# Fewer turns of the identity on the tensor engine in the set-up of a fused decoder layer

## The reference, cut to what matters

```python
x = x + attn(layernorm(x), W_attn, b_attn, W_proj, b_proj)      # 16 heads of 8, rotary factor on q and k, causal
x = x + xattn(ctx, ctx, layernorm(x), Wk, Wv, bv, Wq, bq, Wo, bo)
x = x + ffn(layernorm(x), router_w, w_gate, w_up, w_down, sw_gate, sw_up, sw_down, gate_w)
```

## Time and profile before

| what | us |
|---|---|
| median of 3 runs | 470.13 |
| lowest and highest of the 3 | 468.83, 485.78 |
| the profiled execution's own time | 470.84 |
| its span, first to last instruction | 469.1 |
| PE busy in the span | 407.7 (87%) |
| DVE, ACT, POOL busy | 335.8, 294.8, 258.9 |
| mean granted clock of TensorE | 0.955 |

### The profile page before, as it was taken

One profiled execution on the slowest core, in us unless ns is written; L12 is line 12 of the kernel. 1 busy time (PEld: TensorE's weight loads), 2 busy tenths in 40 slices (PEclk: granted clock), 3 DMA queues, 4 the chain that ended last, 5 costly groups with the idle time before them and its releaser, 6 DMA issues. The chain is left out here.

```text
span 469.1 us, 14511 instructions
## 1 busy us (share of the span) xinstructions
PE 407.7 (87%) x4932; PEld 321.6 (69%) x4932; DVE 335.8 (72%) x1125; ACT 294.8 (63%) x989; POOL 258.9 (55%) x313
## 2 busy tenths in 40 slices
PE   8987999989989898898987866988888889989884
PEld 7655777767667676676666644777777777767673
DVE  6266678899988988878877565856566566656467
ACT  2156699898979889788977654464454444534320
POOL 7834071544857758655445647654555555555453
PEclk9999699999999999999999785899999999999998
DMA  7423022221422313214011261223222323232198
GB/s 200 142 67 138 3 96 79 98 94 44 149 70 69 124 33 115 84 47 146 28 31 42 75 199 47 65 61 77 73 76 76 86 71 79 71 83 61 41 296 241
DMA packets 46712, 43.15 MB, mean 92 GB/s; under 512 B 6320, under 2 KB 38336, under 8 KB 46640
## 3 DMA queue, kind: packets, MB, share of 16 engines
q1 hardware_dynamic: 41150, 32.70, 22.8%
q0 software_dynamic: 4320, 8.99, 5.7%
q10 hardware_dynamic: 1170, 0.53, 0.4%
HBM read 17.26 MB, written 12.09 MB: 63 GB/s over the span
## 5 line engine op out<-in xcount | busy, mean ns | idle before, releaser
L701 POOL DMA_INDIRECT ys<-ctx_t,xload x71 | 68.2, 960 | 57.3 <-ACT ctx_t L1277 41.2
L657 POOL DMA_INDIRECT xs<-xrow,posu x64 | 66.8, 1044 | 21.4 <-issue 11.5
L1159 ACT ACTIVATE probs<-ps_scores 128x512 f32<-128x512 f32 x128 | 72.0, 599 | 3.3 <-PE ps_scores L840 3.3
L1023 PE MATMUL ps_scores<-wide,xe 128*128 x213 | 66.9, 423 | 1.8 <-DVE xe L1589 1.8
L683 POOL TENSOR_SCALAR xrow<-res,mv,rs 128x128 f32<-128x128 f32 x27 | 21.7, 804 | 75.7 <-ACT rs L1207 75.6
L1600 DVE COPY probs<-ps_shared 128x256 f32<-128x256 f32 x71 | 30.0, 423 | 37.9 <-PE ps_shared L1031 23.8
L1382 DVE TENSOR_REDUCE negmax<-ps_scores 128x4 f32<-128x512 f32 x64 | 41.1, 684 | 17.4 <-PE ps_scores L810 16.8
L1267 ACT ACTIVATE xe<-ps_scores 128x128 fp32r<-128x128 f32 x71 | 19.6, 278 | 40.5 <-PE ps_scores L1015 21.6
L1040 PE MATMUL ps_shared<-wd,probs 128*128 x284 | 43.9, 277 | 0.1
L1382 DVE TENSOR_REDUCE negmax<-s_copy 128x4 f32<-128x512 f32 x64 | 42.8, 673 | 0.3 <-ACT s_copy L1153 0.3
L1272 ACT ACTIVATE vst<-ps_scores 128x256 f32<-128x256 f32 x71 | 27.4, 386 | 24.8 <-PE ps_scores L1023 21.4
(11 more groups left out here) (250 smaller groups left out, 1094.3 us busy)
## 6 DMA issues: line engine op xcount, KB each, us to landing
wide<-x_late SPq DMA_DIRECT2D x42, 256.0 KB, 2.5
xload<-xs SPq DMA_DIRECT2D x71, 66.0 KB
wide<-ys SPq DMA_DIRECT2D x8, 512.0 KB, 7.3
ctx_t<-in_ctx SPq DMA_DIRECT2D x32, 64.0 KB
out_x<-res SPq DMA_DIRECT2D x8, 256.0 KB, 3.7
wide<-x_late SPq DMA_DIRECT2D x6, 192.0 KB, 2.3
ys<-ctx_t,xload POOLq DMA_INDIRECT x71
wd<-in_L_ffn_w_down SPq DMA_DIRECT2D x8, 128.0 KB
```

Of the source, the lines that this page charges most:

```text
L657: pool.indirect_dma_start(out=xs, out_offset=bass.IndirectOffsetOnAxis(ap=posu[:, g % 2, k, u:u + 1], axis=0), in_=xrow[:, g % 2, k, u, :] ...
L701: pool.indirect_dma_start(out=ys, out_offset=bass.IndirectOffsetOnAxis(ap=xload_i[:, i % XL, C + 1:C + 2], axis=0), in_=ybuf[:, i % 4, :], ...
L1023: mm = pe.matmul(PS[i % 2][:], a[:, i % 4, :], m[:, bass.ds(e, 1), :].rearrange("p a f -> p (a f)"), start=(r == 0), stop=(r == 2))
L1159: act.activation(probs[:, b % 2, j * HJ:(j + 1) * HJ, :].rearrange("p a t -> p (a t)"), SC[score_bank(("scores_t", b), j)][:], ACT.Exp)\
```

## The change

It shortens two of the rows of identity turns and takes the third away, with the function that only the third used. Nothing else is moved, and no wait is added or taken away.

```diff
-            def free_turns(bank, n):
-
-                for _ in range(n):
-                    pe.transpose(bank[:, 0:128], ident[:], ident[:])
-
...
                 if g == 0 and n == 1:
                     turned_weights()
-                    idle_turns(8)
+                    idle_turns(2)
...
                 if b == 0:
-                    idle_turns(18)
+                    idle_turns(3)
...
                 bank = w.bank_free(("turn_max", b))
-                if b == 0:
-                    free_turns(bank, 14)
                 w.ge(maxed, NJ * (b + 1))
                 pe.transpose(bank[0:NH, 0:T], negmax[:, b % 2, :], ident[:]).then_inc(put_bank(("turn_max", b)), 1)
```

## The result

The changed kernel takes 478.57 us in the median of 4 runs (475.69 to 480.09), the kernel before, run beside it, 470.37 (4 runs). The ratio is 1.0186, 95% interval 1.0126 to 1.0246: slower, by 8 us, against the 6.2 forecast. (A ratio compares only the runs in the faster and more frequent of two states that executions fall into; of the four runs before, the one of 485.78 us is not in it.) Repeats of the whole change gave 1.0135 (1.0082 to 1.0188), 1.0128 (1.0082 to 1.0173) and 1.0115 (1.0053 to 1.0176). They ran on two other chips, on both of which the same kernel before takes 436 to 437 us (the last slots of its pipeline take 6.5 instead of 7.4 us; slots 5 to 14 are the same, and the slots before them differ only with the clock), so absolute times are compared only inside one set of runs.

The account below looks back on a forecast made before the run. It took the early slots' serial loop of TensorE bursts and ACT exponentials as the bound, run at the low clock: 2.0 us late at the exponentials, +2.4 and +1.8 in two slots, sum +6.2, giving 476.3 us, range 468.4 to 483.0.

Parts of the forecast that it names:

- scores(0) at 20.75: First scores burst, set-up: starts about 20.75 instead of 22.24 us, once the six stack moves land at 20.6.
- turn_max(0) at 25.75: Turn of the first row maxima: starts at 25.75 instead of 26.57 us, 0.8 us sooner.
- Which execution: Set-up: step times taken from the one profiled execution, its clock rising at some 21.1 us.
- The one-and-a-half microseconds of part two: Second row cut, 18 to 3 turns, ahead of scores(0): lets it start 1.5 us sooner.
- The folded biases at 0.42 us each: Between turn_max(0) and scores_t(0): four starts 0.42 us apart, 1.7 us together, the same at either clock level.
- The low level through slot 3, and slot 4 at the low level too: Low clock from scores(0) through slot 3, costing +2.4 and +1.8 us in two slots; slot 4 unchanged, 0.
- Part three: Removing the 14 turns before turn_max(0), which started 0.5 us after the maxima were there.
- The first clock record comes after 45 us: Sign that the forecast is right: the trace's first recorded clock change comes after 45 us.
- Rival (a): Early slots: the clock comes up anyway or holds, leaving only the 0.9 us ordering gain, 469.2 us; chance 0.20.
- (a'): Identity turns never raise the clock, so cutting them costs nothing: 469.2 us; chance 0.03.
- Rival (b): Low level outlasts slot 4, 2.0 us per extra slot, 482.3 us with three; chance 0.17.
- Rival (c): Clock rises by slot 2 (+2.0 us) and the dip at 45 us falls away (-2.0): 467 to 470; chance 0.08.

Follow-up runs that it names:

- e4_all: The whole change again, a second execution, against the kernel before: ratio 1.0135 (1.0082 to 1.0188).
- e8_before: The kernel before, unchanged, profiled in another execution: ratio 0.997 (0.9929 to 1.0012).
- e13_before: The kernel before, unchanged, a third execution: ratio 0.9989 (0.9954 to 1.0025).
- e11_all: The whole change, a third execution, against the kernel before: ratio 1.0128 (1.0082 to 1.0173).
- e12_all: The whole change, a fourth execution, against the kernel before: ratio 1.0115 (1.0053 to 1.0176).
- e3_row14: Only the third row of turns taken away, 14 to 0, against the kernel before: ratio 1.0090 (1.0046 to 1.0135).
- e5_thin: Kernel before with the rows of 8 and 18 turns kept in number but turning only 16 identity columns each: ratio 1.0017 (0.9984 to 1.0050).
- e1: Only the first row of turns cut, 8 to 2, against the kernel before: ratio 1.0091 (1.0057 to 1.0125).
- e2: Only the second row of turns cut, 18 to 3, against the kernel before: ratio 1.0088 (1.0037 to 1.0139).
- e6_keep14: First two rows cut (8 to 2, 18 to 3), the 14 turns kept, against the kernel before: ratio 1.0064 (1.0037 to 1.0091).

## Why the prediction was right, and where not

Time, sign and range were right, 476.3 us forecast in 468.4 to 483.0, and so was the named cause: without the turns the first slots run at the low level. The forecast gave 0.18 to more than 2%, and the ratio came at 1.0186. But that the sum hit the number is in large part luck. It put all of its 6.2 us between the set-up and scores(5). There the first pair has 1.1 us, the pairs with equal starts 3.1 and 3.5, and the rest came from where the sum had nothing: in the first pair low stretches of the clock at 216 and 244 us, in the others the end of the program. Step by step, with e4_all, which had the same start as the earlier trace rows to the hundredth of a microsecond until 17.14 us:

```profile
20.73 1.12 PE L798 MATMUL ps_scores<-wide 31*128 31x128 f32 x16 [1.86 <-DMA wide<-x_late]
...
25.89 0.37 PE L819 MATMUL ps_shared<-ident,negmax 128*16 128x128 f32 x1 [2.00 <-DVE negmax L1375]
...
28.54 0.80 PE L746 MATMUL ps_shared<-wpT,probs 128*128 128x128 f32 x2
29.27 0.79 PE L747 MATMUL ps_shared<-rows,one_row 1*128 1x128 f32 x2
...
33.87 1.12 PE L828 MATMUL ps_scores<-wide 32*128 32x128 f32 x16
...
37.70 1.12 PE L798 MATMUL ps_scores<-wide 31*128 31x128 f32 x16
```

- scores(0) at 20.75, ahead of it a wait for the stack moves: measured 20.73. turn_max(0) at 25.75: measured 25.89. Right, for an execution that starts as late as this one.
- "Which execution" is the step that failed for the gain. The prediction took the profiled execution, where the clock rose only at 21.1 us, as the rule. In e8_before and e13_before it rose at 5.9 and 6.8 us, the row ended before the stacks landed, and shortening it gains nothing. The one-and-a-half microseconds of part two were seen only where the clock is late.
- The folded biases at 0.42 us each "at either level": 0.73 at the low level (28.54 to 29.27), four of them 1.2 us more than the sum had. scores_t(0) came at 33.87, not 32.35, and scores(2) 3.55 us later than in the earlier trace rows, not 2.0. The row at the high level had been read as a bound that does not depend on the clock.
- The low level through slot 3, and slot 4 at the low level too: it ended sooner, at 41.5 (e4_all), 36.6 (e11_all), 34.5 (e12_all) and 38.8 us (after), in slot 1 or 2. The slots priced at 7.90 each took 7.16 and 6.98 in e4_all, and slot 4, priced at the 9.40 of before, 5.73. With these the lateness at scores(5) is 57.56 - 55.08 = 2.5 us for this start, where the sum had 6.2; the pairs with an early start have 3.1 (e11_all, e8_before) and 3.5 (e12_all, e13_before). The statement that nothing in these slots is dense enough to raise the clock was wrong: in e4_all it rose in slot 2, behind project(1, 1), the burst and the values.
- Part three, about -0.4 us of order: it was a cost of its own, 0.9% alone. The prediction saw the wait of turn_max(0) and not that without the turns in it the engine would stand idle for 2 us and the clock stay low for 14 us (e3_row14, 19.0 to 32.7). With it alone scores(5) came 3.0 us later than in e5_thin, as much as with the whole change. This is the largest missing term.
- "The first clock record comes after 45 us": wrong in all four executions, it came at 11.5, 5.9, 7.2 and 41.5 us.
- What the profile of before was read for held: e4_all's clock column reads 1.00 from 20 to 40 us while its bursts take 1.5 us, since its record begins at 41.5.

```profile
20.00:25.00 5.00, 3.15 (x38) 1.00 0.76 267
25.00:30.00 5.00, 4.11 (x42) 1.00 0.32 87
```

Rival (a), the clock comes up or holds, did not happen in any of the four executions (it fell at 18.4, 16.1 and 17.5 us, and in e4_all it had not been up before 41.5); (a'), the rule of the Trainium skill ("TensorE: Matmul & The Clock Gate", section on the PE-mode transpose) that transposes do not engage full speed, is contradicted by e1, e2 and e3, each slower by 0.9% for nothing but transposes taken away, and by e8_before, where TensorE did hardly anything but the fourteen turns between the fall at 19.6 us and the rise at 23.0. Rival (b) had a point in the first profile, but by stretches far behind slot 4, which the repeats don't show. Rival (c) had half of it: the clock did rise by slot 2, and in three of the four executions the stretch near 45 us shrank to 3.4 us.

Left open: the spans of e4_all, e11_all and e12_all end 4.26 us after the issue of their last store, those of e8_before, e13_before and e6_keep14 2.7 us. These 1.5 us are a quarter to a third of the difference on chips B and C. They are not the store's, which lands 2.29 us after its issue in all of them. They come by POOL: its last addition (line 706) ends at 431.3 us in e11_all against 426.2 in e8_before, 5.1 us later where the last store is issued only 3.4 later, and in both the span ends 7.3 to 7.4 us behind it. In the three slower ones the second of the loads that these additions wait for (line 561) also lands 2.4 to 2.7 us behind the first, in e8_before and e13_before 1.5. The profile of the change on chip A doesn't have the long end, and e5_thin, with all 40 turns, has it. Why it comes was not tried.

## What to carry to other kernels

Before an engine's filler work is cut, look what stands in its place: here it was a wait of 2 to 3 us in front of a stretch in which the tensor engine is on the path, and the filler was worth its time, also where it seemed only to fill a wait. And read more than one execution before a step is priced from where the clock changes: the kernel before had its first rise at 5.9, 6.8 and 21.1 us in three executions, which moved scores(0) by 5 us and decided whether a row of turns was in the way at all. A clock column that reads full speed before its first change says nothing; the spacing of equal instructions does.

## What the runs showed of the hardware that was not expected

With 26 of the 40 turns replaced by turns of 16 columns, the clock rose and fell within 0.3 us of where it does with turns of 128, and the time stayed (ratio 1.0017, interval 0.9984 to 1.0050). Pairs of fp32 matmuls with 128 columns that stood 0.42 us apart at the high level stood 0.73 us apart at the low one, while the turns went from 0.11 to 0.21 us. And of three chips one ran the same kernel in 468 us and two in 436 to 437, with equal slots in the first half of the pipeline and, in the second, some of 7.9 against 7.3 and of 7.4 against 6.5 to 6.7 us; why was not tried.
